# Repeats of the line features: columns reordered, three of the four copies written by ScalarE and one by VectorE

## What is computed

```python
def _plucker_lines(p1, p2):
    parts = [p1[..., i] * p2[..., j] - p1[..., j] * p2[..., i] for i, j in _PAIRS]
    lines = jnp.stack(parts, axis=-1)                    # 6 numbers a token and head
    n = jnp.linalg.norm(lines, axis=-1, keepdims=True)
    return lines / jnp.maximum(n, 1e-12)
...
q = _plucker_lines(q1, q2).transpose(0, 2, 1, 3)
k = _plucker_lines(k1, k2).transpose(0, 2, 1, 3)
logits = jnp.einsum('bhtc,bhsc->bhts', q, k @ _J6.T) * _SCALE      # 16 heads, 6 features each
attn = jax.nn.softmax(jnp.where(causal, logits, -jnp.inf), axis=-1)
```

## Time and profile before

| what | value |
|---|---|
| median of 3 runs | 1010.12 us (1009.05 to 1015.84) |
| the profiled execution | 1010.27 us, of which the span between first and last instruction is 1008.5 us |
| granted TensorE clock, mean | 0.885 |
| PE, DVE, ACT, POOL busy | 767.6, 704.4, 588.6, 628.5 us |
| first stage | about 650 us, some 37.6 us a batch |

### The profile page before, as it was taken

The page is one execution under the profiler, slowest core; times in us unless marked ns, Lnnn a source line. Parts: engine busy times, 40 slices in busy tenths (PEclk is TensorE's granted clock), DMA queues, the critical chain, the costliest instruction groups (busy, mean ns, idle before and its releaser), DMA issues.

```text
span 1008.5 us, 24870 instructions
## 1 busy us (share of the span) xinstructions
PE 767.6 (76%) x7672; PEld 481.7 (48%) x7673; DVE 704.4 (70%) x1858; ACT 588.6 (58%) x907; POOL 628.5 (62%) x914
## 2 busy tenths in 40 slices
PE   3468878879879879889879878667989989899100
PEld 2324444444444445344434434365878778788000
DVE  1665688797797787788788785476756656666394
ACT  0177677576576677567567668333456656666145
POOL 4155456686686686677676676525076666666594
PEclk9579899899899889889889889698999999999655
DMA  5000000110110110111011011325333333332483
GB/s 182 12 1 11 12 22 27 39 43 27 38 42 26 37 42 26 37 39 42 24 42 35 18 43 54 106 82 153 98 101 95 104 102 88 98 98 68 128 254 123
DMA packets 95055, 66.03 MB, mean 65 GB/s; under 512 B 9052, under 2 KB 87654, under 8 KB 94992
## 3 DMA queue, kind: packets, MB, share of 16 engines
q1 hardware_dynamic: 69328, 39.77, 14.0%
q0 software_dynamic: 8768, 17.07, 5.1%
q10 hardware_dynamic: 16896, 8.39, 2.8%
HBM read 34.50 MB, written 31.74 MB: 66 GB/s over the span
## 4 chain that ended last, share of the span: by engine, by line
PE 42%; DVE 34%; issue 11%; ACT 5%; POOL 3%; DMA 2%; SPq 2%; ACTq 1%; DVEq 1%; POOLq 0%
PE S L870 12%; PE O L690 8%; PE O L886 6%; PE W L655 5%; PE S L675 3%; DVE prodA L1218 3%; DVE rs_a L1242 2%; PE W L631 2%; DVE rs_b L1241 2%; DVE x L1294 1%; ACT p L1001 1%; DVE prodA L1223 1%; ACT probs L1016 1%; PE W L901 1%; DVE rden L1269 1%
## 5 line engine op out<-in xcount | busy, mean ns | idle before, releaser
L1016 ACT ACTIVATE probs<-S 128x1024 f32<-128x1024 f32 x320 | 322.8, 1033 | 171.0 <-PE S L675 124.2
L546 POOL TENSOR_SCALAR_AFFINE_SELECT probs<-probs 128x256 f32<-128x256 f32 (+1 forms) x448 | 220.6, 517 | 183.9 <-ACT probs L1016 183.1
L589 POOL DMA_INDIRECT z_scratch<-y,rows x144 | 146.4, 1016 | 100.5 <-ACT y L1104 63.2
L690 PE MATMUL O<-probs,v_aug 128*32 128x512 f32 (+3 forms) x2048 | 184.7, 482 | 4.7 <-POOL probs L546 4.7
L247 POOL DMA_INDIRECT rows_scratch<-xrow,slot_i x128 | 132.0, 1032 | 57.6 <-issue 32.1
L675 PE MATMUL S<-qkT 32*128 32x512 f16 (+3 forms) x1024 | 144.1, 323 | 14.9 <-ACT probs L1016 9.0
L1532 DVE TENSOR_TENSOR hid<-hid 128x512 f16<-128x512 f32 x104 | 72.0, 692 | 95.0 <-ACT hid L1131 94.2
L1112 ACT ACTIVATE silu<-S 128x512 f32<-128x512 f32 x104 | 62.1, 597 | 116.9 <-PE S L870 115.0
L870 PE MATMUL S<-xT_rt,w_T 128*128 128x256 f16 x864 | 107.9, 275 | 16.3 <-DVE xT_rt L1489 8.2
L886 PE MATMUL O<-w_T,hid 128*128 (+1 forms) x1248 | 96.8, 222 | 11.9 <-DVE hid L1532 10.5
L655 PE MATMUL W<-ident,feat 128*128 128x128 f16 x512 | 55.5, 276 | 57.1 <-DVE rt_logit L1311 40.5
(11 more groups left out here) (155 smaller groups left out, 1203.7 us busy)
## 6 DMA issues: line engine op xcount, KB each, us to landing
rows<-rows_scratch SPq DMA_DIRECT2D x72, 130.0 KB, 2.2
z<-z_scratch SPq DMA_DIRECT2D x32, 256.0 KB, 4.0
x_in<-in_L_attn_x ACTq DMA_DIRECT2D x16, 256.0 KB, 2.8
x_scratch<-x SPq DMA_DIRECT2D x16, 256.0 KB, 2.3
x1T_scratch<-x1T SPq DMA_DIRECT2D x16, 256.0 KB, 2.3
xT_sh<-x1T_scratch SPq DMA_DIRECT2D x32, 128.0 KB, 3.1
x_in<-x_scratch SPq DMA_DIRECT2D x32, 128.0 KB, 3.3
out<-res ACTq DMA_DIRECT2D x16, 256.0 KB, 2.9
```

Source lines behind the costliest of these rows:

```text
L546: pool.affine_select(out=v, in_=v, compare_op=ALU.is_ge, fill=0.0, base=0, pattern=[[0, v.shape[1]], [1, P]], channel_multiplier=-1).then_ ...
L589: pool.indirect_dma_start(out=z_dram, in_=y[:, q, a, :], in_offset=None, out_offset=bass.IndirectOffsetOnAxis(ap=rows[:, q, a, P + 1:P + 2 ...
L690: mm = pe.matmul(O[g % 2][32 * j:32 * j + 32, kb * P:T], v_aug[:, par, kb, 4 * g + j, :], probs[:, g % 2, c, col:col + T - kb * P], start= ...
L1016: act.activation(probs[:, g % 2, c, :], S[(g + c) % 2][:, :], ACT.Exp, scale=-SCALE / SPLIT_UP ** 2).then_inc(s_exp, 1)
```

## The change

The columns of a feature row are reordered. The q rows become [hi, hi, lo, lo], the k rows [hi, lo, lo, hi] stay as they were in content, but are written in another way: the low half now goes to piece 2, for q and k together. That leaves q's piece 1 (hi) and k's piece 3 (hi), which can be written once the high half is there, and k's piece 1 and q's piece 3 (lo). ACT writes the first three of these in a new function `repeat_features`, DVE the last. `feat_done` is now counted to two for a batch, once by ACT and once by DVE. Two new semaphores, `feat_hi` and `feat_lo`, say that the two halves are written; `feat_lo` takes the place of `prodB_read` too.

```diff
+        def piece(n, side=None):
+            f = feat[:, :, :].rearrange("p (s h) l -> p s h l", s=2)[:, :, :, n * LINE:(n + 1) * LINE]
+            return f.rearrange("p s h l -> p (s h) l") if side is None else f[:, side]
...
                 if g == 0:
-                    pe.wait_ge(feat_done, c + 1)
+                    pe.wait_ge(feat_done, 2 * (c + 1))
...
+            def repeat_features(c):
+                act.wait_ge(feat_hi, c + 1)
+                act.copy(piece(1, 0), piece(0, 0))
+                act.copy(piece(3, 1), piece(0, 1))
+                act.wait_ge(feat_lo, c + 1)
+                act.copy(piece(1, 1), piece(2, 1)).then_inc(feat_done, 1)
...
                 exps(b, 2, (4,))
-                exps(b, 3, (0, 1))
+                exps(b, 3, (0,))
+                if not last:
+                    repeat_features(b + 1)
+                exps(b, 3, (1,))
...
                 dve.wait_ge(featT_full, HP * c)
-                chain(dve.tensor_copy(feat[:, :, 0:LINE], prodB[:, :, :]))
-                dve.tensor_tensor(feat[:, :, LINE:2 * LINE], prodB[:, :, :], feat[:, :, 0:LINE], ALU.subtract)\
-                    .then_inc(prodB_read, 1)
-                dve.wait_ge(prodB_read, c + 1)
-                f = feat[:, :, :].rearrange("p (s h) l -> p s h l", s=2)
-                dve.tensor_copy(f[:, 0, :, 2 * LINE:4 * LINE], f[:, 0, :, 0:2 * LINE])
-                dve.tensor_copy(f[:, 1, :, 2 * LINE:3 * LINE], f[:, 1, :, LINE:2 * LINE])
-                dve.tensor_copy(f[:, 1, :, 3 * LINE:4 * LINE], f[:, 1, :, 0:LINE]).then_inc(feat_done, 1)
+                dve.tensor_copy(piece(0), prodB[:, :, :]).then_inc(feat_hi, 1)
+                dve.wait_ge(feat_hi, c + 1)
+                dve.tensor_tensor(piece(2), prodB[:, :, :], piece(0), ALU.subtract).then_inc(feat_lo, 1)
+                dve.wait_ge(feat_lo, c + 1)
+                dve.tensor_copy(piece(3, 0), piece(2, 0)).then_inc(feat_done, 1)
```

More of the change, by code:

```diff
@@ L183, in block_program @@
         pts_full = sem("pts_full"); pts_read = sem("pts_read"); val_full = sem("val_full"); val_read = sem("val_read")
-        prodB_done = sem("prodB_done"); prodB_read = sem("prodB_read")
+        prodB_done = sem("prodB_done"); feat_hi = sem("feat_hi"); feat_lo = sem("feat_lo")
         feat_done = sem("feat_done"); featT_full = sem("featT_full"); featT_read = sem("featT_read")
@@ L531, in line_products @@
                 pool.wait_ge(pts_read, 2 * (c + 1))
-                pool.wait_ge(prodB_read, c)
+                pool.wait_ge(feat_lo, c)
                 for dst, many, one in products(prodB, 0, 1):
@@ L999, in copy_points @@
                     act.wait_ge(prodB_done, NPROD * c)
-                    act.wait_ge(prodB_read, c)
+                    act.wait_ge(feat_lo, c)
                 act.copy(p12[:, :, :, 2 * half:2 * half + 2].rearrange("p a s t h c -> p (a s) t (h c)"),
@@ L1048, in _ @@
             copy_values(0, 0)
+            repeat_features(0)
             def raise_weights(b, k):
@@ L1430, in lower_weights @@
                                              op1=ALU.subtract).then_inc(w_lo, 1)
-            per = 4 + (4 + 12 + 2) + 2 + 2 + 13 + 3
+            per = 4 + (4 + 12 + 1) + 2 + 2 + 13 + 3
             base[0] = count[0]
```

## The result

The changed kernel takes 1013.09 us (median of 20 runs, 1007.21 to 1022.23) against 1007.70 us (20 runs, 998.57 to 1017.20) of the kernel before on the same chip: ratio 1.0066, 95% interval 1.0046 to 1.0086. That is slower, by less than 1%: 5.4 us between the medians. The profiled execution took 1012.48 us, 2.2 us more than that of the kernel before, so the two traces show less than half of the difference.

A forecast was written before the change was run, and what follows sets the result against it. In the first stage PE waits for DVE's feature copies, unless ACT is late. Gains of 9.9 us less losses of 9.4, and 2.4 for the clock, took 1010.27 to 1012 us, range 1000 to 1021.

The forecast's parts named there:

- 1.35 us behind the exponential (3, 0): Earliest release of PE where ACT is late: three copies on ACT behind that exponential, plus 0.06 us to PE; bounds 0.87 to 1.59.
- 0.64 behind the subtraction: Release where ACT is free: 0.64 us after DVE's subtraction, from 0.05 + 0.53 for ACT's copy + 0.06 to PE.
- rival 1: ACT never decides the release, or PE makes good its losses: 1000 us, or 993 with 1.13 us in all fifteen; 18%.
- rival 4: ACT's copies are as long as DVE's blocked ones, so every release stays where it was: 1010 us; 7%.
- Which decides: Releases of features 4, 6, 10, 12, 15 follow the subtraction, gaining 1.13 us each; features 5, 7, 8, 9, 13, 14 follow ACT.
- The losses of features 1 to 3: Releases in the first batches, where exponential (3, 0) ends late: losses of 2.98, 0.57 and 3.23 us, counted in full.
- Features 11: Release at 450.06 us, where PE ran at low clock ahead and ACT would allow 452.72: a loss of 2.66 us.
- Gains and losses cancel: Over all releases of the first stage, gains of 9.9 us against losses of 9.4: 0.5 us to the good.
- The clock: New waits of about 3 us at features 1, 3 and 11 bring PE's low clock; one of three costs 2.4 us.
- rival 2: Shorter waits at eleven releases no longer bring the low clock, 2.4 us back each: half 999 us, all 986; 7%.
- Rival 3: ACT's lateness spreads to two or more further batches of the loop, with low clock behind all three late ones: 1029 us; 13%.
- the blocking that the prediction had beside its sum: POOL's masking may block DVE's remaining copy, release 0.80 us after the subtraction, not 0.64: 0.8 us less gain, range only.

## Why the prediction was right, step by step

It gave 1012 us, range 1000 to 1021, no change, and the measurement is 1013.09. That the two are so close is in part luck: it started from a profiled execution of 1010.27 us, and the median of the kernel before came out at 1007.70, so the change itself was forecast at 1.9 us and measured at 5.4 (4.6 to 8.7 by the interval). What it had right is the mechanism, that the wait goes to ACT's last copy and gains and losses nearly cancel, and that the rest stays under 1%. Its steps:

- **The copy on ACT** was taken at 0.53 us; it measured 0.517 to 0.525. **The copy left on DVE** was taken at 0.36 and measured 0.371.
- **1.35 us behind the exponential (3, 0)** where ACT decides: 1.28 to 1.37 in 13 of 15 releases. **0.64 behind the subtraction** where it doesn't: 0.69 in features 4 and 15. PE waits for ACT at all 16 releases, so rival 1 fell, and the copies are short, so rival 4 did. They take 0.50 to 0.53 us whether POOL is masking or not.
- **Which decides.** This is where the working was off. Features 6, 10 and 12, taken for the subtraction's with a gain of 1.13 us each, turned out to be ACT's: in the trace after, the subtraction of features 6 ends 0.40 us behind (3, 0) (267.61 and 267.21), and not 1.07, so the release comes 0.97 us behind the subtraction where it had been 1.77: 0.80 instead of 1.13. In features 7 it was 0.61 against a forecast of 0.63.
- **The losses of features 1 to 3** were taken at 2.98 + 0.57 + 3.23 = 6.8 us. Measured at the releases: 3.22 us later at features 1, 4.34 at features 2, 7.56 at features 3. The program's start was 1.68 us ahead at features 0, and that was lost as well by features 1, where (3, 0) ended at 75.67 us in the one trace and 75.44 in the other. **Features 11** were to lose 2.66; they aren't of the late kind any more (the copies follow (3, 0) there as in features 7). Features 13 are of the late kind in their place: (3, 0) ends at 528.15, 1.9 us behind DVE's copy, and the batch takes 40.19 us. What the two share is a second low stretch of the clock in the middle of the batch ahead of them: about 6.8 us ahead of features 11 before, 3.4 ahead of features 13 after, from 520 us on:

```profile
520.00:523.50 3.50, 3.50 (x20) 1.29 (x20) 3.19 (x10) 2.71 (x3) 2.33 (x5) 0.58 0.31 113
```

- **Gains and losses cancel.** From features 3 to 15 the lateness falls from 7.56 to 3.14 us, 4.4 won, where the sum had 5.6 + 4.0 - 2.66 = 6.9. In the sum of PE's standing the cancelling is there: 57.0 to 56.3 us, 0.7 less, where 0.5 was forecast. The forecast in all, 0.5 us to the good and 2.4 us of clock, is 1.9 to the bad; it is 2.2 between the two traces and 5.4 between the medians.
- **The clock.** The waits of 2.64 us still bring the low level, as assumed: 0.66 to 0.69 over the next 10 us behind most releases. But behind features 5, 9 and 13 it is a shorter stretch, a part of what rival 2 had. Summed over features 1 to 14, the time from the release to the next x grows by 3.3 us, where the prediction took 2.4 as one of three new low stretches: behind features 1, 3 and 11 it costs 1.1, 2.1 and 2.7 us, all three, and behind 5, 9 and 13 it gives 1.1, 1.1 and 1.3 back. So the term is right in size and made up otherwise. The windows of the changed kernel from the release of features 7, and of features 9, to the next x (us, then PE, PEld, DVE, ACT, POOL busy, PEclk, DMA share, GB/s):

```profile
305.75:315.86 10.11, 9.70 (x84) 4.65 (x84) 4.18 (x15) 4.77 (x6) 4.46 (x9) 0.67 0.04 13
...
380.02:388.80 8.78, 8.37 (x84) 3.98 (x84) 4.10 (x15) 4.78 (x6) 4.46 (x9) 0.81 0.04 15
```

  Both follow a wait of 2.65 us. The batches behind the shorter stretches are 35.4 to 35.5 us long, the others mostly 36.8 to 37.5. A part of the 7.2 us won back by features 11 is thus the clock's: 9.86 and 8.77 us are the stretches behind features 9 before and after.
- **Rival 3**, that ACT's lateness spreads over the batches, had 13% and lost on the first chip, with one late batch besides the first three (features 13, against features 11 before). On the second chip it is what happens: nearly all batches are late, and 1.033 is more than its 1029 us would be (1.019). The point from which it decides was given as (3, 0) ending later than 0.6 us ahead of the release of before; there it ends 0.2 us behind in features 7. So the rule was right and the chance rested on one chip's trace: with another chip the forecast of no change would have been 3.3% off, and that the result came from the first was luck.

What the experiments show: with the copies behind (3, 0), PE's wait follows ACT's last copy, whatever DVE has been spared; the high copies ahead of (3, 0) cost two thirds of what they cost behind it (1.5% against 2.3%, one chip), and ahead of (2, 4) nothing that could be measured (another chip). In all of these the new order of the columns is included, which by itself costs 0.85% on a third. That the first chip's waits of 3.3 to 4.1 us would be worth something to a kernel with the early copies was not measured, since none of these ran on a chip of that kind.

## What to carry to other kernels

Moving work to the engine with idle time moves the wait too, unless it is put where its input is ready and nobody waits for what comes behind it: kernels with the same two copies take 2.3%, 1.5% or 0.1% more than the kernel before, by their place in ACT's order (the last on another chip). Read from the trace, for each release, when the receiving engine reaches that place, not how busy it is over the span; and ask by how much it would have to be later for the sum to turn, because on another chip it may be. Here (3, 0) had to end 1.4 us later in features 7 (2.0 us ahead of the release, 0.6 the point); on the second chip it ended 1.9 us later, and gain turned to loss.

## What the runs showed that was not expected

- On three chips PE starts the second half of the scores (1, 4) 1.4 us late, in 11 to 13 batches of each trace there and never on the first chip. It waits for the semaphore of its own first half, and the semaphore is what comes late. It is not the loading of code: in the trace of the kernel before on the second chip the instruction queues move nothing between 254 and 562 us, and eight of the stalls lie there. A count over the semaphore events of that trace finds 155 signals of PE more than 1.2 us behind the start of their matmul, 106 of them in the second stage, and 4 in the trace of the first chip.
- The kernel before takes 1083 to 1098 us on these chips against 1008; its second stage, from the last exponential to the end, takes 462.9 us against 361.9. The late signals lie in the second stage too, but that they are its 101 us isn't shown, and what holds them up is open.
- The same wait of 2.64 us of PE is followed by 10.1 us at a granted clock of 0.67 or by 8.8 us at 0.81, in the same kernel and the same batches' work. It isn't settled what picks one; the short one ends 1.3 us sooner each time.
- DVE's copies of the same 384 elements had means of 613 and 443 ns on the first chip and 306 and 315 ns in the trace of the same kernel on the second. What differs is POOL. Beside a masking (L546) the copies are long: L1257 below lasts until 0.1 us behind the end of the third. Beside L247, by which POOL issues a DMA, it takes 0.25 us (292.15, shown above). The rows of the kernel before on the first chip, features 7, and then on the second:

```profile
297.14 1.53 POOL L546 TENSOR_SCALAR_AFFINE_SELECT probs<-probs 128x256 f32<-128x256 f32 x3
298.10 0.69 DVE L1257 COPY feat<-feat 128x384 f16<-128x384 f16 x1
...
291.93 0.98 POOL L247 DMA_INDIRECT rows_scratch<-xrow,slot_i  x1 [0.17 <-ACT probs L1016]
```

  This is the blocking that the prediction had beside its sum; the longest such copy, at features 10, took 1.06 us. So the 1.65 us from the subtraction to the release, of which the change wanted to win most, were 1.06 us there before anything was changed.
